# Another order of the attention stage: maxima two batches and projections three batches ahead, all exponentials inside their batch, value products between the cosines

## The reference, cut to what matters

```python
Q, K, V = x @ Wq + bq, x @ Wk + bk, x @ Wv + bv        # 8 heads of 16
qq, kq = Q @ Wc2q + bc2q, K @ Wc2q + bc2q              # 8 numbers a head
fid = dots(qq, kq) / maximum(norm(qq) * norm(kq), 1e-8)
qw = fid * (1.0 + 0.1 * sin(fid * pi))
aw = 0.5 * qw + 0.5 * (Q @ K.T / sqrt(16))
probs = softmax(aw, axis=-1)
heads = probs @ V
```

## Time and profile before

| | |
|---|---|
| median of 3 runs | 550.81 us (550.0 to 550.89) |
| profiled execution | 552.67 us, its span 550.9 us |
| busy in the span | PE 393.9, DVE 368.5, ACT 339.8, POOL 267.0 us |
| mean granted TensorE clock | 0.889 of full speed |
| attention, first sine of a batch | batch 10 at 229.22, batch 11 at 243.98 |
| DMA | 58.19 MB, mean 106 GB/s |

### The profile page before, as it was taken

How to read it: one execution, slowest core, us unless ns; L and a number is a source line. 1 busy time by engine, 2 the same in 40 slices (tenths; PEclk the granted TensorE clock), 3 DMA queues, 4 the chain that set the end, 5 groups by cost and what they waited for, 6 DMA issues and landing times.

```text
span 550.9 us, 9018 instructions
## 1 busy us (share of the span) xinstructions
PE 393.9 (72%) x2668; PEld 282.0 (51%) x2668; DVE 368.5 (67%) x887; ACT 339.8 (62%) x715; POOL 267.0 (48%) x399
## 2 busy tenths in 40 slices
PE   0978688888888888888888788664000399999960
PEld 0754366555555555555555433663000288888850
DVE  4886557788888888888888524549983016666670
ACT  0244346788898888888888735864210277778740
POOL 8364016444444444444440012374877207787874
PEclk9979859899999999999999989967555589999995
DMA  9560203355445555555552899900111215666500
GB/s 210 29 153 20 60 23 88 89 136 137 117 117 138 134 133 121 128 126 131 130 122 67 106 140 132 237 5 11 35 40 54 80 39 155 199 192 201 175 14 0
DMA packets 81245, 58.19 MB, mean 106 GB/s; under 512 B 17619, under 2 KB 72919, under 8 KB 81196
## 3 DMA queue, kind: packets, MB, share of 16 engines
q1 hardware_dynamic: 75142, 53.12, 44.3%
q0 software_dynamic: 2496, 4.29, 2.3%
q10 hardware_dynamic: 3558, 0.20, 0.5%
HBM read 35.38 MB, written 23.11 MB: 106 GB/s over the span
## 4 chain that ended last, share of the span: by engine, by line
PE 35%; issue 21%; DVE 15%; ACT 14%; SPq 9%; POOL 2%; DMA 2%; ACTq 1%; POOLq 0%; DVEq 0%
PE ps L1559 8%; DVE mxs L1719 7%; PE ps L1570 7%; ACT big L920 5%; SPq L518 4%; ACT big L910 4%; SPq L557 3%; DVE big L1798 3%; PE ps L1374 3%; PE ps L1367 3%; PE ps L1387 3%; PE ps L1352 2%; PE ps L1229 2%; ACT proj L861 2%; DVE gb L1633 1%
## 5 line engine op out<-in xcount | busy, mean ns | idle before, releaser
L1719 DVE TENSOR_REDUCE mxs<-ps 128x4 f32<-128x1024 f32 x64 | 76.6, 1218 | 21.5 <-PE ps L1229 20.4
L1768 DVE SCALAR_TENSOR_TENSOR big<-big,ps 128x1024 f32<-128x1024 f32 x64 | 74.6, 1216 | 2.5 <-ACT big L910 2.5
L910 ACT ACTIVATE big<-ps 128x1024 f32<-128x1024 f32 x64 | 61.9, 1012 | 7.4 <-PE ps L1352 7.2
L694 POOL CAST mtok<-mxs 128x8 bf16<-128x8 f32 x32 | 6.0, 189 | 115.1 <-DVE mxs L1719 115.1
L1798 DVE TENSOR_TENSOR big<-big,ps 128x1024 f32<-128x1024 f32 x32 | 38.9, 1216 | 25.5 <-PE ps L1374 25.5
L811 POOL DMA_INDIRECT out_dram<-arena,fidx x46 | 46.7, 1016 | 17.9 <-issue 16.4
L1352 PE MATMUL ps<-proj 128*128 128x256 f16 x256 | 40.7, 286 | 19.4 <-DVE mxs L1719 14.1
L1229 PE MATMUL ps<-arena 96*128 96x256 bf16 x256 | 39.1, 276 | 18.5 <-ACT big L920 13.9
L2104 DVE TENSOR_SCALAR arena<-ps,x_all 128x128 f32<-128x128 f32 x46 | 14.0, 347 | 56.8 <-PE ps L1579 48.8
L1559 PE MATMUL ps<-arena,big 128*128 128x256 f32 x184 | 47.2, 403 | 1.1 <-ACT arena L1125 1.1
L1119 ACT ACTIVATE x_all<-x_all 128x128 f32<-128x128 f32 x46 | 20.1, 486 | 44.2 <-DMA x_all<-sorted_rows 42.0
(11 more groups left out here) (341 smaller groups left out, 963.7 us busy)
## 6 DMA issues: line engine op xcount, KB each, us to landing
big<-in_L_ffn_w_dram SPq DMA_DIRECT2D x46, 256.0 KB
qk_parts<-proj SPq DMA_DIRECT2D x16, 384.0 KB, 3.2
arena<-qk_parts SPq DMA_DIRECT2D x32, 192.0 KB, 3.5
sorted_rows<-zrow SPq DMA_DIRECT2D x16, 266.0 KB, 3.7
arena<-qk_parts SPq DMA_DIRECT2D x32, 128.0 KB, 4.0
proj<-u_parts SPq DMA_DIRECT2D x48, 64.0 KB
x_all<-sorted_rows SPq DMA_DIRECT2D x23, 133.0 KB
sorted_rows<-zrow SPq DMA_DIRECT2D x2, 1263.5 KB, 26.8
```

The costliest lines, as they stand in the source:

```text
L910: nc.scalar.activation(W[par][:, n, :], src, ACT.Sin, scale=PI * (1 - 1e-6)).then_inc(sin_ready, 1)
L1719: nc.vector.tensor_reduce(mxs[:, b1 % 2, :, 2 * n:2 * n + 2], src, AX_X, ALU.max, negate=True).then_inc(unit_free, 1)
L1768: nc.vector.scalar_tensor_tensor(W[par][:, n, :], W[par][:, n, :], 10.0, f, ALU.add, ALU.mult).then_inc(unit_free, 1)
```

## The change

Only orders, their counters and their waits change. Maxima units now run for batch b + 2 inside batch b, and the projection of batch b + 3 (QK0 = 3) instead of b + 2; so batch 2 is projected, copied and split in the setup (bank 4 of PSUM, `make_qk(2)` and `take_qk(2)` in the second group of the setup loop, `split_qk(2)` before `split_u(0)`, `put_qk(2)` and `get_qk(2)` behind those of batch 1), and all eight maxima units of batches 0 and 1 run before the first cosine. Cosines, sines and weights go in the order 0, 1, 3, 2. All four exponentials of a batch are taken in that batch, in the order 0, 1, 3, 2. The value products of b - 1 stand before and behind cosine 2. The two turned maxima of b + 1 both run in batch b. Waits that counted by n count by the place of n in `sin_order`; `get_qk` and `get_u` wait for the latest of the four units.

```diff
         th = tbank.bitcast(FP16)
 
-        turns = [("u", 0), ("u", 1), ("m0", 0)]
+        QK0 = 3
+        turns = [("u", 0), ("u", 1), ("m0", 0), ("m1", 0)]
+        turns_before = []
         for b in range(NB):
-            turns += [("m1", b)] + [(k, b + d) for k, d in (("qk", 2), ("u", 2), ("m0", 1)) if b + d < NB]
+            turns_before.append(len(turns))
+            turns += [(k, b + d) for k, d in (("qk", QK0), ("u", 2), ("m0", 1), ("m1", 1)) if b + d < NB]
         turn_no = {k: i for i, k in enumerate(turns)}
 
-        units = [("max", 0, n) for n in range(HP)]
+        sin_order = (0, 1, 3, 2)
+        units = [("max", b, n) for b in range(2) for n in range(HP)]
         for b in range(NB):
-            units += [("cos", b, n) for n in range(HP)]
-            for k, d, n in (("log", 0, 0), ("max", 1, 0), ("log", 0, 1), ("max", 1, 1), ("log", 0, 2), ("log", 0, 3), ("max", 1, 2), ("max", 1, 3)):
+            units += [("cos", b, n) for n in sin_order]
+            for k, d, n in (("log", 0, 1), ("log", 0, 0), ("log", 0, 3), ("max", 2, 3), ("max", 2, 2), ("log", 0, 2), ("max", 2, 0), ("max", 2, 1)):
                 if b + d < NB:
                     units.append((k, b + d, n))
...
+            for r in range(2):
+                put_max(0, r)
+                get_max(0, r)
 
             def body(b, par, first, last, slow):
-                put_max(b, 1)
-                if 2 <= b + 1 < NB:
-                    get_u(b + 1)
-                get_max(b, 1)
-                zeros(ZA)
+                if b + QK0 < NB:
+                    put_qk(b + QK0)
                 if b + 2 < NB:
-                    put_qk(b + 2)
                     put_u(b + 2)
                 if not last:
                     put_max(b + 1, 0)
+                    put_max(b + 1, 1)
+                    get_max(b + 1, 0)
+                if b + QK0 < NB:
+                    get_qk(b + QK0)
+                if not last:
+                    get_max(b + 1, 1)
                 if b + 2 < NB:
-                    get_qk(b + 2)
-                if not last:
-                    get_max(b + 1, 0)
+                    get_u(b + 2)
+                zeros(ZA)
...
                 nc.gpsimd.tensor_tensor(bA_bc[:, :], bA_bc[:, :], small[:, 0:NQ], ALU.add).then_inc(set_cp, 1)
 
             def body(b, par, first, last, slow):
-                split_max(b, 1)
+                if not last:
+                    split_max(b + 1, 0)
                 if b + 2 < NB:
                     split_u(b + 2)
-                    split_qk(b + 2)
                 if not last:
-                    split_max(b + 1, 0)
+                    split_max(b + 1, 1)
+                if b + QK0 < NB:
+                    split_qk(b + QK0)
                 xb = x_all[:, b * TPB:(b + 1) * TPB, :]
                 nc.gpsimd.tensor_tensor(xb, xb, mv_all[:, 0, b * TPB:(b + 1) * TPB].unsqueeze(2).to_broadcast([P, TPB, C]), ALU.subtract)
                 if first:
                     root_out()
...
-                if first and slow:
+                if first:
                     take_max(0, 0)
+                    take_max(0, 1)
                 sin(0)
-                if first and not slow:
-                    take_max(0, 0)
                 sin(1)
-                take_max(b, 1)
+                sin(3)
+                if b + QK0 < NB:
+                    take_qk(b + QK0, tbank)
                 sin(2)
-                sin(3)
                 if first:
                     weights(1)
+                else:
+                    heads_out(b - 1)
+                exp(b, par, 0)
+                if first:
+                    weights(2)
                 if b + 2 < NB:
-                    take_qk(b + 2, tbank)
-                if not first:
-                    exp(b - 1, 1 - par, HP - 1)
-                for n in range(HP - 1):
-                    exp(b, par, n)
-                    if first:
-                        weights(n + 2)
-                    if first and n == HP - 2:
-                        nc.scalar.activation(hT[:, 0:1], halfpi[:, 0:1], ACT.Sin)
-                    if n == 0 and b + 2 < NB:
-                        take_u(b + 2)
-                    if n == 1 and not first:
-                        heads_out(b - 1)
-                    if n == 1 and not last:
-                        take_max(b + 1, 0)
+                    take_u(b + 2)
+                exp(b, par, 1)
+                if first:
+                    weights(3)
+                exp(b, par, 3)
+                if not last:
+                    take_max(b + 1, 0)
+                exp(b, par, 2)
+                if first:
+                    weights(4)
+                    nc.scalar.activation(hT[:, 0:1], halfpi[:, 0:1], ACT.Sin)
+                if not last:
+                    take_max(b + 1, 1)
                 if last:
...
                     max_unit(0, 3)
-                if first and slow:
                     turn_max(0, 0)
-                if slow:
-                    norm_rows()
-                cos_unit(0)
-                if first and not slow:
-                    turn_max(0, 0)
-                cos_unit(1)
-                cos_unit(2)
-                turn_max(b, 1)
-                cos_unit(3)
-                if first:
-                    weights_1()
-                if b + 2 < NB:
-                    bank_free("qk", b + 2)
-                    make_qk(b + 2, tbank)
-                logit_unit(0)
-                if not last:
-                    max_unit(b + 1, 0)
-                if first:
-                    weights_2()
-                logit_unit(1)
-                if b + 2 < NB:
-                    turn_u(b + 2)
+                    max_unit(1, 0)
+                    turn_max(0, 1)
+                    for n in range(1, HP):
+                        max_unit(1, n)
                 if b == 1:
                     pe.wait_ge(w_act, 4)
                 if b == 2:
                     pe.wait_ge(set_cp, 3)
                     pe.wait_ge(w_dve, 2)
+                if slow:
+                    norm_rows()
+                cos_unit(0)
+                cos_unit(1)
+                if b + QK0 < NB:
+                    bank_free("qk", b + QK0)
+                    make_qk(b + QK0, tbank)
+                cos_unit(3)
                 if not first:
                     pv(b - 1, 1 - par, 0)
-                if not last:
-                    max_unit(b + 1, 1)
+                cos_unit(2)
+                if first:
+                    weights_1()
+                else:
+                    pv(b - 1, 1 - par, 1)
+                logit_unit(1)
+                logit_unit(0)
+                if first:
+                    weights_2()
+                logit_unit(3)
+                if b + 2 < NB:
+                    turn_u(b + 2)
+                    max_unit(b + 2, 3)
+                    max_unit(b + 2, 2)
                 if first:
                     weights_3()
-                logit_unit(2)
-                if not first:
-                    pv(b - 1, 1 - par, 1)
-                logit_unit(3)
                 if not last:
                     turn_max(b + 1, 0)
-                if not first:
-                    heads_back(b - 1)
+                logit_unit(2)
+                if b + 2 < NB:
+                    max_unit(b + 2, 0)
                 if not last:
-                    max_unit(b + 1, 2)
+                    turn_max(b + 1, 1)
                 if first:
                     weights_4()
-                if not last:
-                    max_unit(b + 1, 3)
+                else:
+                    heads_back(b - 1)
...
                 dve.wait_ge(unit_ready, unit_no["max", b1, n] + 1)
-                if n % 2 == 0 and b1 >= 2:
-                    dve.wait_ge(m_split, 4 * (b1 - 2) + n + 2)
+                if b1 >= 2:
...
                 if first:
                     top(0, 2)
                     top(0, 3)
+                    for n in range(HP):
+                        top(1, n)
                 if slow:
                     norms()
-                for n in range(HP):
+                for n in sin_order:
                     weight(n)
                 if first:
                     own_steps[0] = before_batches
-                if not last:
-                    top(b + 1, 0)
+                logits(1)
                 if first:
                     weights_2()
-                logits(1)
-                if not last:
-                    top(b + 1, 1)
+                    root_out(1)
+                logits(3)
                 if first:
-                    root_out(1)
                     weights_3()
-                logits(3)
+                if b + 2 < NB:
+                    for n in (3, 2, 0, 1):
+                        top(b + 2, n)
                 if not first:
                     heads(b - 1)
-                if not last:
-                    top(b + 1, 2)
-                    top(b + 1, 3)
                 if last:
```

(24 more changed lines are left out.)

45 lines of the change are left out of this document (25 added, 20 removed).

## The result

The changed kernel takes 523.22 us (median of 4 runs, 520.75 to 523.23) where the kernel before takes 550.4 (median of 4, 549.93 to 550.89): ratio 0.9495, 95% interval 0.9465 to 0.9524. Predicted were 520.6 us and a range of 516.5 to 531. The profiled execution took 523.22 us with a span of 521.5; before it was 552.67, so the two profiles differ by 29.4, against 30.2 predicted.

What follows compares the result with a forecast made beforehand. The order of operations, not the work, was taken to bound the kernel. First sine of batch 1 to last heads: 188.3 - 222.4, plus 3.9 for batch 0, gives -30.2; 550.81 becomes 520.6 us, range 516.5 to 531.

Steps and rivals of the forecast that it cites:

- The layout of a batch: Steady batch laid out on every engine and queue: 12.40 us if ScalarE never waits, taken as 12.5; 14.76 before.
- half fit: Steady batches: ScalarE waits once or twice more, likeliest for logits 2; 13.3 a batch, 531 us in all; chance 0.18.
- first sine of batch 1: End of batch 0: this sine comes 3.9 us later than the 95.57 of before, ends 2 and 6.
- Late maxima: Second maxima load, behind six big loads, holds up logits 3; 555 us at a landing of 7.0; chance 0.03.
- 7.8 + L: Length per batch of the maxima loop, L being the load's landing; hidden up to L = 4.6 us.
- never seen above its 3.3 of cover: Claim about the second maxima load: before the change its landing L never exceeded 3.3 us of cover.
- TensorE waiting for a DMA at logits 3: Sign that the prediction is wrong: TensorE waits for a load at maxima 3 or logits 3.
- Batch 0: Four more maxima units and reductions ahead of the first weight: 4 x 1.14 = 4.6 us later; the rest with the same durations.
- The clock rival: TensorE stays at 1.2 GHz through the seam into batch 1; some 5 us lost, 526 us; chance 0.06.
- Setup: Batch 2's projection, copy and split move here: GpSimd's split of 3.75 us fits its 4.58 wait; 0 taken, 1.8 if uncovered.
- What follows attention shifts whole: Code behind the last heads is the same, released by them, and moves with them without changing length.
- The drain: A table switch costs ScalarE about 1.38 us beyond the load: 15.16 a batch, 558 us in all; chance 0.01.

Runs made afterwards that it cites:

- a2: Changed kernel plus one unused 1024-column VectorE reduction in each of 14 batches, ahead of reduction 0: 530.08 us, ratio 0.9624.
- a1: Changed kernel plus one unused 512-column ScalarE copy per batch, right ahead of the heads copy: 527.32 us, ratio 0.9591.
- r1: Changed kernel with both value products put back behind the logits and the heads copy behind exponential 2: 549.36 us, ratio 0.9971.
- r2: Changed kernel with only value product 1 put back behind logits 2 and the heads copy behind exponential 2: 534.86 us, ratio 0.9717.
- after_again: Changed kernel itself, unedited, run again on one chip beside a variant with an earlier second maxima load: 519.96 us, ratio 0.9471.
- n1: Changed kernel with cosines, sines and weights in the order 0, 1, 2, 3, exponentials still 0, 1, 3, 2: 519.26 us, ratio 0.9445.
- p1: Kernel before, old depths, with exponentials inside their batch, value products between cosines ahead of the projection, heads copy ahead of exponential 0: 548.08 us, ratio 0.9969.

## Why the prediction was right, and what it missed

**The layout of a batch.** It said 12.40 if ScalarE never waits, and the batch takes 12.39 to 12.41. It said that the heads copy and logits 3 would lose their waits, that VectorE would be idle some 0.3 ahead of the first weight (0.17 shown, 0.44 by a2), and TensorE occupied 11.4 (the profile counts 11.95 as busy, its ends being modelled). a1 shows that ScalarE's sequence is the length. The "half fit" rival did not come: in the steady batch ScalarE waits for no logits. One sentence on the old order is wrong: both value products do not stand between logits 2 and 3. The earlier trace rows has 16 matmuls there, one product; the other stood ahead of maxima 1. r1 and r2 show that either place cost 0.8.

**The sum, term by term.** Times of the first sines: batch 1 at 97.92, batch 2 at 111.25, batch 13 at 248.73; the last heads end at 286.56.

| term | predicted | measured |
|---|---|---|
| first sine of batch 1 | +3.9 | +2.35 |
| batch 1 | 13.3 | 13.33 |
| batches 2 to 12 | 137.5 | 137.48 |
| batch 13 | 12.1 | 12.27 |
| batch 14 | 11.8 | 11.80 |
| batch 15 to the last heads | 13.6 | 13.76 |
| first sine of batch 1 to last heads | 188.3 | 188.64 |
| behind the last heads | 0 | +2.0 |
| all | -30.2 | -29.4 |

Three of these matches are luck. The 137.48 is ten batches of 12.40 and one of 13.53, where the prediction spread 0.1 over each for small waits. What cost something was another thing, the maxima. Batch 1 was predicted as 12.5 and the 0.8 by which the old batch 1 was longer than its followers. In the old one TensorE's clock was granted at 0.89 and at the lower level for 3.4 us; how much of the 0.8 that made was not separated:

```profile
95.57:111.16 15.59, 12.37 (x105) 8.61 (x104) 10.97 (x11) 12.79 (x17) 7.38 (x15) 0.89 0.41 106
```

In the new one it was granted at 1.00, and what batch 1 has above 12.40 is its own wait for the maxima, as shown above. And in the sum, batch 0 (1.55 too much) and the rest (2.0 too little) nearly cancel. Of the 2.6 by which the median missed, 0.8 is the sum; the other 1.9 is that the prediction took the profiled execution to lie 1.9 above the median, and this time it was the median.

**Late maxima.** As a rival it was given 0.03 and counted harmless up to a landing of 4.6 us. The mechanism was right, the slack was mis-sized, in two terms of its 7.8 + L. The formula took `get_max 0` 0.3 us behind the second maxima copy, as if the write of the first half had always landed by then. In the other steady batches that write took 1.2 to 1.7; for batch 11 it took 3.27, and `get_max 0` left 2.15 behind the copy. And from the start of logits 3 to the end of the next second maxima copy it is 4.76 (230.26 to 235.02), where the formula has 0.65, 1.26 and 2.5, together 4.41, and 0.13 more pass between landing and start. So the loop is 8.3 + L and is hidden up to a landing of 4.1; with the 1.71 and the landing of 3.51 it gives the 13.5 of the long batch. The landing was also taken too short: "never seen above its 3.3 of cover" does not hold for the trace before, where the same transfer behind six loads took up to 3.57. The wait of batch 1 is not in this loop. It comes from batch 0, where the copy is late, and it returned in after_again (1.37) and n1 (1.49), while the late write did not. (What was late there, once each, in a steady batch, was SyncE, which took 3.8 us from `get_max 0` to `get_max 1`.) Of the prediction's own signs of being wrong, "TensorE waiting for a DMA at logits 3" did come, in these two batches.

**Batch 0.** The step for the four more units was about right: the first weight starts at 77.58 instead of 73.61, and the first reductions of this execution had started 0.88 earlier than before, so 4.85 for the 4.6 predicted. The mis-sized term is what follows: from there to the first sine of batch 1 it took 20.3 us where it was 22.0. TensorE's clock was at its lower level from 70.0 to 76.8 and from 87.0 to 93.8 (0.62 granted from 73 to 78, 1.00 from 78 to 84, 0.74 from 84 to 97). Before, it was there from 69.9 to 83.6, as long in all, in one piece. So 6.8 of the 20.3 us ran at the lower level and 10.0 of the 22.0; the order of operations changed as well, and what is owed to which was not separated. How much this level weighs, the ten executions of the kernel after and its edits show. From the first sine of batch 0 to that of batch 1 they take 19.4 us where none of it ran at the lower level (four), 20.3 to 20.5 where 5.7 to 6.0 us did (five, a2 with its extra work among them), and 21.4 where 7.1 did, which is the execution above. The first sine of batch 1 came at 97.92 to 99.50 in all ten; the predicted sign was 98 to 101.

**The clock rival** was wrong in its place: batch 1 ran at 1.00. In r1 it came elsewhere, in the batch of 15.57, where TensorE had waited 0.89, 0.52 and 0.52 ahead of the fall, as it does in every batch of r1.

**Setup.** No cost is left of it in the end: the first reductions start 0.88 earlier than before. The split of batch 2 takes 3.75 us of GpSimd's wait, as said:

```profile
44.06 1.16 POOL L663 TENSOR_TENSOR proj<-proj 128x512 bf16<-128x512 f32 x1
47.43 0.87 POOL L675 TENSOR_TENSOR proj<-u_sb,inv 128x256 f32<-128x256 f32 x1 [2.21 <-DVE inv L1691]
```

The wait of 4.58 in the earlier trace rows became 2.21 behind the split. The two do not add up to 4.58, since VectorE's root came later. VectorE's four operations ahead of it took 2.92 beside the split, and 1.11 earlier, while GpSimd stood idle. Before, the same four took 1.10. First the kernel after, then before:

```profile
37.32 1.11 DVE L1656 TENSOR_SCALAR gb<-x_all,mv_all 128x128 f32<-128x128 f32 x4
...
41.14 2.92 DVE L1656 TENSOR_SCALAR gb<-x_all,mv_all 128x128 f32<-128x128 f32 x4
```

```profile
41.71 1.10 DVE L1633 TENSOR_SCALAR gb<-x_all,mv_all 128x128 f32<-128x128 f32 x4
```

The prediction had this at nothing. Later waits of VectorE took it up.

**"What follows attention shifts whole"** failed as a step. It took 2.0 us longer in the profiled execution than before, the same instructions. Nothing of it comes from the first half: the kernel after is up to 1.6 us behind for a while, but VectorE's first operation of the experts starts 131.3 us behind the last heads in both, since a longer wait takes the difference up. The kernel after, then before:

```profile
417.83 0.61 DVE L2125 TENSOR_SCALAR arena<-ps,x_all 128x128 f32<-128x128 f32 x2 [29.71 <-PE ps L1602]
```

```profile
449.32 0.61 DVE L2104 TENSOR_SCALAR arena<-ps,x_all 128x128 f32<-128x128 f32 x2 [31.40 <-PE ps L1579]
```

The 2.0 is lost among the experts. Two waits of VectorE there are 2.41 and 2.95 where they were 1.13 and 1.31, and ahead of the first of them ScalarE waits for the sorted rows of a tile, 2.44 where it was 1.13:

```profile
432.90 0.88 ACT L1140 ACTIVATE x_all<-x_all 128x128 f32<-128x128 f32 x2 [2.44 <-DMA x_all<-sorted_rows]
```

Why they are longer was not found. after_again spent 231.6 on the whole rest, so this is a spread between executions and not shown to be a cost of the change.

**The drain.** The table load ends at 216.67 and the exponential starts at 216.68; from load to operation it is 1.29, and from the end of the heads copy to the load 0.01. The rule of the Trainium skill (ScalarE: Activation LUTs, What ACT_TABLE_LOAD costs), a drain of about 1.38 us more at each switch, does not hold in this trace: by it the batch would have been 15.16, an estimate from the page's figure.

**The expectations of r1 and p1** missed in the same way. They took away or gave back a wait and left the others as they were. In r1 two products out of place made waits on ScalarE and VectorE of 0.45 to 1.29, and in p1 the wait that was gone gave its place to another (for the projection). The prediction had laid out all engines for the whole batch and came within 0.01 with its 12.40 (the sum then took 12.5); the two guesses by single waits missed, p1 by 1.2 us a batch and r1 by 9 us and more in all.

## What to carry to other kernels

When three engines are each busy for over 80% of a period and none for all of it, lay out one whole period by hand from the durations of the trace, every engine, every slot and every queue, and look for the order in which the longest engine never waits: it is worth doing whole, since half of such a reordering may be worth a third of it or nothing (0.79, 0.69 and, in p1, 0 of 2.36 here). Count each load's cover from the write that it depends on, that write's landing included, and to the start of the unit that waits for it (0.37 us to spare here). Look at the first periods by themselves: their order is not that of the steady ones. Judge such edits by the period, which repeated within 0.02 us in undisturbed batches, and not by the total, whose untouched part scattered by 5.5.

## What was not expected of the hardware

- A write of 4 KB to memory landed 1.2 to 1.7 us after its issue in nearly all of the steady batches' writes. For batch 11 it took 3.27 (first half) and 2.3 (second half), for batch 12 3.26 (second half), with the DMA engines at 0.71 of their share. A read of 4 KB landed after 1.3 to 1.5 us ahead of the six loads of the projections, and after 2.9 to 3.9 behind them.
- The same instructions behind the last heads took 229.4 to 234.9 us in thirteen profiled executions; TensorE's granted clock there goes between 0.5 and 0.9 in the slices of the page.
- The same four operations of VectorE took 1.1 us while GpSimd was idle and 2.9 beside a GpSimd split.
- With the same work and order, batch 0 took 19.4 to 21.4 us, by how much of it fell on the lower level of TensorE's clock.
- Merged rows hide short waits: four operations of VectorE took 4.69 with such waits and 4.60 without. With the visible 0.17 that is 0.26 of the 0.44 that a2 found.
